# A decoder layer in one kernel: the output projection as three split passes, with its weights in the ring

## What is computed

```python
x = x + attn(layernorm(x), W_Q, b_Q, W_K, b_K, W_V, b_V, W_O, b_O)
x = x + xattn(layernorm(x), k, fside, ctx, ctx, 8)
x = x + ffn(layernorm(x), ...)

def attn(x, ...):
    Q, K, V = x @ W_Q + b_Q, x @ W_K + b_K, x @ W_V + b_V   # per head, float32
    scores = rope(Q) @ rope(K).T / sqrt(128)
    probs = softmax(where(causal, scores, -inf))
    z = probs @ V
    return einsum('bqnd,ndm->bqm', z, W_O) + b_O
```

## Time and profile before

| | us |
|---|---|
| timed runs, median of 3 | 995.27 (993.92 to 996.04) |
| the profiled execution | 985.83 |
| its span | 983.8 |
| TensorE busy in the span | 949.0 |
| VectorE, ScalarE, GpSimd busy | 723.6, 379.0, 408.5 |

### The profile page before, as it was taken

How to read it: one execution, slowest core, us unless ns; L and a number is a source line. 1 busy time by engine, 2 the same in 40 slices (tenths; PEclk the granted TensorE clock), 3 DMA queues, 4 the chain that set the end, 5 groups by cost and what they waited for, 6 DMA issues and landing times.

```text
span 983.8 us, 18292 instructions
## 1 busy us (share of the span) xinstructions
PE 949.0 (96%) x6081; PEld 836.6 (85%) x6081; DVE 723.6 (74%) x1523; ACT 379.0 (39%) x1063; POOL 408.5 (42%) x320
## 2 busy tenths in 40 slices
PE   7999999999999999999999999888999999999996
PEld 6788888988898888888898888777888799999985
DVE  6878967877877889667888777646777666666647
ACT  3546443442234643233544333431352344444420
POOL 1312313163521245563225365306706366666660
PEclk9999999999999999999999999989999999999999
DMA  7863397321079922236877501350142477777768
GB/s 268 306 238 138 118 354 288 147 87 65 1 246 368 356 87 72 80 103 219 298 261 244 198 35 45 135 233 26 67 172 78 95 121 121 119 118 120 119 113 297
DMA packets 64841, 161.17 MB, mean 164 GB/s; under 512 B 6640, under 2 KB 40304, under 8 KB 63600
## 3 DMA queue, kind: packets, MB, share of 16 engines
q1 hardware_dynamic: 50304, 140.97, 40.6%
q0 software_dynamic: 14448, 19.05, 11.9%
HBM read 84.72 MB, written 75.27 MB: 163 GB/s over the span
## 4 chain that ended last, share of the span: by engine, by line
PE 86%; issue 4%; DVE 4%; POOL 2%; ACT 2%; DMA 1%; SPq 0%; DVEq 0%; ACTq 0%
PE bank L487 12%; PE bank L489 11%; PE bank L488 11%; PE bank L717 11%; PE bank L735 6%; PE bank L567 6%; PE bank L863 4%; PE bank L865 3%; PE bank L553 3%; PE bank L590 3%; PE bank L592 3%; PE bank L591 2%; POOL xs L1208 2%; PE bank L834 2%; PE bank L824 2%
## 5 line engine op out<-in xcount | busy, mean ns | idle before, releaser
L1200 POOL TENSOR_TENSOR rot<-turn 128x512 f32<-128x512 f32 x64 | 94.2, 1472 | 283.6 <-DVE rtotal L1357 216.2
L1368 DVE SCALAR_TENSOR_TENSOR turn<-bank,bqk,trig 128x1024 f32<-128x1024 f32 x128 | 162.2, 1279 | 29.0 <-PE bank L489 26.0
L1263 POOL DMA_INDIRECT sums<-ysb,token_at x79 | 123.1, 1558 | 69.5 <-DVE ysb L1736 35.2
L1230 POOL TENSOR_TENSOR kv<-c_t,v_t 128x512 f32<-128x512 f32 x64 | 67.8, 1071 | 134.6 <-PE bank L592 69.0
L717 PE MATMUL bank<-wo,z_t 128*128 128x256 f32 x512 | 116.0, 379 | 0.8 <-ACT z_t L1066 0.8
L487 PE MATMUL bank<-xt_hi,w_hi 128*128 128x512 f32 x256 | 105.3, 411 | 1.7 <-DVE xt_lo L1332 1.7
L717 PEld LDWEIGHTS bank<-wo,z_t 128*128 128x128 f32 x512 | 94.9, 190 | 12.8 <-ACT z_t L1066 1.0
L1058 ACT COPY prob_t<-bank 128x512 f32<-128x512 f32 x64 | 37.5, 586 | 163.3 <-PE bank L553 163.3
L489 PE MATMUL bank<-xt_hi,w_lo 128*128 128x512 f32 x256 | 100.1, 391 | 0.0
L1024 ACT ACTIVATE prob<-prob,negmax 128x128 f32<-128x128 f32 x256 | 99.0, 390 | 2.5 <-DVE negmax L1353 2.4
L488 PE MATMUL bank<-xt_lo,w_hi 128*128 128x512 f32 x256 | 99.7, 390 | 0.0
(11 more groups left out here) (181 smaller groups left out, 2285.7 us busy)
## 6 DMA issues: line engine op xcount, KB each, us to landing
xs<-zeros SPq DMA_DIRECT2D x16, 2120.0 KB, 13.6
w_hi<-w_dram SPq DMA_DIRECT2D x24, 768.0 KB, 4.3
w_lo<-w_dram SPq DMA_DIRECT2D x24, 768.0 KB, 7.2
xe_all<-xs SPq DMA_DIRECT2D x79, 132.5 KB, 2.6
sums<-zeros SPq DMA_DIRECT2D x3, 2176.0 KB, 18.3
raw<-in_wqkv SPq DMA_DIRECT2D x16, 384.0 KB, 4.2
w_dram<-w_hi SPq DMA_DIRECT2D x8, 768.0 KB, 6.6
w_dram<-w_lo SPq DMA_DIRECT2D x8, 768.0 KB, 8.5
```

The source lines that it names most:

```text
L1200: nc.gpsimd.tensor_tensor(rot[m][1][:], turn[m][1], turn[m][2], ALU.add).then_inc(rot_pool, 1)
L1263: nc.gpsimd.indirect_dma_start(sums_dram[s % SUMS], bass.IndirectOffsetOnAxis(ap=token_at[:, s:s + 1], axis=0), ysb[s % YBUFS][:], None, c ...
L1368: last = nc.vector.scalar_tensor_tensor(turn_all[m][:, 2 * i:2 * i + 2, :], qk_bank[2 * m + i][:].unsqueeze(1).to_broadcast([128, 2, GT]), ...
```

## The change

- The output projection becomes three fp32r passes over z_hi, z_lo, wo_hi and wo_lo: 24 matmuls of 256 columns in a step.
- ScalarE writes the weighed values with their bias to prob_t, which it has just finished with, and casts them from there to z_hi. GpSimd subtracts to get z_lo (`z_low`), first thing in its step. ScalarE's next copy into prob_t waits for it.
- wo is no longer loaded in whole. Two heads of it (128 x 512) are a third chunk of each pair's weights, in the same raw buffers; the list CHUNKS gives the order. The chunk that comes with pair q belongs to the output projection of pair q - 2. It is stored with the pair (wo_dram) and loaded again with it, so a pair is now 2 MB where it was 1.5 MB. The reload of a place waits for the output projection too. Two more loads come in the tail.
- Of the four kv products of a step of GpSimd the last two move into the next step, behind the low parts.

```diff
+CHUNKS = [(0, 0), (0, 1), (1, 0), (1, 1), (0, CH), (1, CH)] + [(p, c) for p in range(2, PAIRS) for c in range(CH + 1)]
             for p in range(PAIRS):
-                for c in range(CH):
+                while n < len(CHUNKS) and CHUNKS[n][0] <= p and (p or CHUNKS[n] in ((0, 0), (0, 1))):
+                    q, c = CHUNKS[n]
                     if n >= 2:
                         sp.wait_ge(w_hi_done, n - 1)
                         sp.wait_ge(w_lo_done, n - 1)
-                    sp.dma_start(raw[n % 2][:], wqkv_in[p, c]).then_inc(raw_loaded[n % 2], 16)
+                    if c < CH:
+                        sp.dma_start(raw[n % 2][:], wqkv_in[q, c]).then_inc(raw_loaded[n % 2], 16)
+                    else:
+                        sp.dma_start(raw[n % 2][:, 0:2 * D], wo_in[wo_pair(q)]).then_inc(raw_loaded[n % 2], 16)
                     n += 1
...
                     sp.wait_ge(v_ready, 2 * (PAIRS * (g - 1) + W_BEFORE[p] + 1))
+                    sp.wait_ge(wo_done, PAIRS * (g - 1) + W_BEFORE[p] - 1)
...
+                    load_wo(p)
...
-                    pe.wait_ge(zt_taken, s * 2 - 4)
...
+                    at = W_AT[(p - 1) % PAIRS]
+                    pe.wait_ge(z_hi_done, s * 2 - 4)
+                    pe.wait_ge(z_lo_done, s * 2 - 4)
...
                         for h in range(2):
-                            last = nc.tensor.matmul(
-                                acc[b // 2][:, (b % 2) * D:(b % 2 + 1) * D], z_t[h][:, b, :],
-                                wo[:, 2 * r + h, :], start=(r == 0 and b % 2 == 0 and h == 0),
-                                stop=(r == PAIRS - 1 and h == 1), skip_group_check=True)
+                            nc.tensor.matmul(o, z_hi[h][:, b, :], wo_hi[:, at, h, :],
+                                             start=(r == 0 and b % 2 == 0 and h == 0), stop=False, skip_group_check=True)
+                            nc.tensor.matmul(o, z_hi[h][:, b, :], wo_lo[:, at, h, :],
+                                             start=False, stop=False, skip_group_check=True)
+                            last = nc.tensor.matmul(o, z_lo[h][:, b, :], wo_hi[:, at, h, :], start=False,
+                                                    stop=(r == PAIRS - 1 and h == 1), skip_group_check=True)
...
-                                act.wait_ge(zt_ready, s * 2 - 6 + h + 1)
+                                act.wait_ge(z_lo_done, s * 2 - 6 + h + 1)
...
-                            nc.scalar.activation(z_t[h][:], zt_bank[:].rearrange("p (b n) -> p b n", b=GB),
+                            nc.scalar.activation(prob_t[h][:], zt_bank[:].rearrange("p (b n) -> p b n", b=GB),
                                                  ACT.Identity, bias=bv[:, n:n + 1]).then_inc(zt_taken, 1)
...
+                            nc.scalar.copy(z_hi[h][:], prob_t[h][:]).then_inc(z_hi_done, 1)
...
                 if first and p < PAIRS - 1:
-                    split_hi(2 * p + 2)
-                    split_hi(2 * p + 3)
+                    for n in range(3 * p + (3 if p else 2), 3 * p + 6):
+                        split_hi(n)
...
+            def z_low(g, p, live):
+                s = g * PAIRS + p
+                for h in range(2):
+                    pool.wait_ge(z_hi_done, s * 2 - 4 + h + 1)
+                    nc.gpsimd.tensor_tensor(z_lo[h][:], prob_t[h][:], z_hi[h][:].bitcast(F32),
+                                            ALU.subtract).then_inc(z_lo_done, 1)
+
             def core_step(g, p, live, first):
                 s = g * PAIRS + p
+                if live(2):
+                    z_low(g, p, live)
+                    if g > 0 and live(0) and 3 <= p < 7:
+                        for f in range(2, 4):
+                            cross_kv(g - 1, 4 * (p - 3) + f)
...
-                    for f in range(4):
+                    for f in range(2):
                         cross_kv(g - 1, 4 * (p - 2) + f)
...
                 if first and p < PAIRS - 1:
-                    split_lo(2 * p + 2)
-                    split_lo(2 * p + 3)
+                    for n in range(3 * p + (3 if p else 2), 3 * p + 6):
+                        split_lo(n)
```

More of the change, by code:

```diff
@@ L56, with wo_pair @@
 EARLY = EXPERTS // 2
+CHUNKS = [(0, 0), (0, 1), (1, 0), (1, 1), (0, CH), (1, CH)] + [(p, c) for p in range(2, PAIRS) for c in range(CH + 1)]
+def wo_pair(q):
+    return (q - 2) % PAIRS
 def shared_bank(k, i):
@@ L150, in decoder @@
         prob_t = [sb(f"prob_t{h}", [128, GB, SEQ], c=tctx) for h in range(2)]
-        z_t = [sb(f"z_t{h}", [128, GB, SEQ], c=tctx) for h in range(2)]
-        wo = sb("wo", [128, HEADS, D], c=tctx)
+        z_hi = [sb(f"z_hi{h}", [128, GB, SEQ], F32R, tctx) for h in range(2)]
+        z_lo = [sb(f"z_lo{h}", [128, GB, SEQ], F32R, tctx) for h in range(2)]
+        wo_hi = sb("wo_hi", [128, WRING, 2, D], F32R, tctx)
+        wo_lo = sb("wo_lo", [128, WRING, 2, D], F32R, tctx)
         bqk = sb("bqk", [128, PAIRS, 4], c=tctx)
@@ L231, in decoder @@
         small_loaded = sem("small_loaded")
-        wo_loaded = sem("wo_loaded")
+        z_hi_done = sem("z_hi_done")
+        z_lo_done = sem("z_lo_done")
         raw_loaded = [sem(f"raw_loaded{i}") for i in range(2)]
@@ L426, in _ @@
                         sp.dma_start(ctxg[:], ctx_in[:, g * GB:(g + 1) * GB, :]).then_inc(ctx_loaded, 16)
+            for p in range(2):
+                sp.wait_ge(wo_done, PAIRS * (GROUPS - 1) + W_BEFORE[p] - 1)
+                load_wo(p)
             sp.wait_ge(v_ready, 2 * PAIRS * GROUPS)
@@ L969, in split_hi @@
                 act.wait_ge(raw_loaded[n % 2], 16 * (n // 2 + 1))
-                p = n // CH
-                if p >= WRING and n % CH == 0:
-                    act.wait_ge(w_stored[W_AT[p]], 32 * W_NTH[p])
+                p, c = CHUNKS[n]
+                if p >= WRING and c == 0:
+                    act.wait_ge(w_stored[W_AT[p]], 64 * W_NTH[p])
                     act.wait_ge(v_ready, 2 * (p - WRING) + 2)
-                nc.scalar.copy(w_hi[:, W_AT[p], n % CH, :], raw[n % 2][:]).then_inc(w_hi_done, 1)
+                if c < CH:
+                    nc.scalar.copy(w_hi[:, W_AT[p], c, :], raw[n % 2][:]).then_inc(w_hi_done, 1)
+                else:
+                    if p > WRING + 1:
+                        act.wait_ge(wo_done, p - WRING - 1)
+                    nc.scalar.copy(wo_hi[:, W_AT[p]], raw[n % 2][:, 0:2 * D].rearrange("p (h n) -> p h n", h=2)).then_inc(w_hi_done, 1)
             def route_exp(g):
@@ L1319, in split_lo @@
                 dve.wait_ge(w_hi_done, n + 1)
-                at = W_AT[n // CH]
-                nc.vector.tensor_tensor(w_lo[:, at, n % CH, :], raw[n % 2][:],
-                                        w_hi[:, at, n % CH, :].bitcast(F32), ALU.subtract).then_inc(w_lo_done, 1)
+                p, c = CHUNKS[n]
+                at = W_AT[p]
+                if c < CH:
+                    nc.vector.tensor_tensor(w_lo[:, at, c, :], raw[n % 2][:], w_hi[:, at, c, :].bitcast(F32),
+                                            ALU.subtract).then_inc(w_lo_done, 1)
+                else:
+                    nc.vector.tensor_tensor(wo_lo[:, at], raw[n % 2][:, 0:2 * D].rearrange("p (h n) -> p h n", h=2),
+                                            wo_hi[:, at].bitcast(F32), ALU.subtract).then_inc(w_lo_done, 1)
             def step(g, p, live, first):
```

46 lines of the change are left out of this document (28 added, 18 removed).

## The result

| | before | after |
|---|---|---|
| timed runs, median | 994.6 us | 1047.23 us (1046.52 to 1048.23) |
| ratio after to before | | 1.0533 [1.0517, 1.0549] |
| the profiled execution, its span | 985.83, 983.8 us | 1048.23, 1046.1 us |

The change costs 52.6 us. The forecast was 26.8 us, with a range that ended at 1040 us: right in sign, half the size.

The account below looks back on a forecast made before the run. TensorE, a full queue from 50 to 620 us, was taken as the bound. Group 0's stall +29.4, clock +10.5, gain -14.5 and tail +1.4 made +26.8 us on a median of 995.27: 1022.1 us, range 1003 to 1040.

Parts of the forecast that it names:

- The stall of group 0: Group 0: the third chunk's load waits for a raw buffer, holding ScalarE's copy and TensorE; +29.4 us before the clock.
- The clock: Group 0: TensorE's idle gaps lower its clock; 1.75 us for each of six waits, +10.5 us, bounds 0 and 20.
- 21.1 us: Group 0: forecast step length, from one transposition of the probabilities to the next, against 16.89 us before.
- I cost it at nothing: Group 0: raw loads A or B queued behind longer stores and loads have almost a whole step; 0 us.
- Rival 2: Group 0's wait is there, but the clock holds or the load lands at 2.4 us: 1010 us; chance 0.22.
- rivals 1 and 4: 1: wait hidden, gain comes through, 981 us, chance 0.08. 4: half the wait covered, 993 to 997 us, chance 0.03.
- GpSimd in the steps with scatters: Groups 2 and 3, steps 5 to 7: added low parts just fit before the rotation; zero, other end +1 us each.
- The gain: Output projection: 24 passes take 2.88 us instead of 3.46; 0.58 us a step, -14.5 us over 25 steps.
- I count 24 + 1 = 25: Steps credited with the shorter output projection: 24 in groups 1 to 3, one in the tail; none in group 0.
- TensorE has other waits there: Tail: the last output projections' wait for cast and subtraction doesn't decide; gus_hi on ScalarE moves back, +1.4 us.
- The forecast profile: Signs: ScalarE idle before wo_hi, TensorE idle at low clock, group 0 longer, groups 1 to 3 shorter, shorter output projection.
- Rival 3: Heavier: load lands at 4.2 us (+9.6), clock (+10) or GpSimd late (+6); two together 1038 to 1048; chance 0.17 over 1033.

Follow-up runs that it names:

- e2: The changed kernel with a third raw buffer, alive only in group 0: 999.6 us, ratio 1.0045 to the kernel before.
- e5: The changed kernel with 16 more matmuls in each of steps 2 to 7 of group 0, ahead of TensorE's wait: 1035.77 us, ratio 1.0429.
- e3: The changed kernel with GpSimd's wait for scattered rows moved behind z_lo in groups 2 and 3: 1034.77 us, ratio 1.0401.
- e4: The changed kernel with both a third raw buffer and the wait for scattered rows behind z_lo: 986.01 us, ratio 0.9912.
- e8: The changed kernel with third raw buffer and moved wait for scattered rows, run again in more rounds: 984.73 us, ratio 0.9915.
- e6: The kernel before, with the wait for scattered rows moved behind the next step's first rotation in groups 2 and 3: 990.41 us, ratio 0.9968.
- e1: The kernel before, unchanged, profiled once more: 994.84 us, ratio 0.9997.

## Why the prediction was wrong

It added up to +26.8 us, and +52.6 was measured. Three terms carry the difference.

**The stall of group 0: mechanism right, +39.9 forecast (29.4 and 10.5 for the clock), 47.6 measured at T(8).** What came true: T(2) 43.69 (forecast 44.1), the landing 2.8 us (2.6), the cast and the copy behind it, TensorE's wait of 4.6 to 6.9 us (4.8), and removal of the one cause removes all of it (e2). Size by size:
- The clock, 10.5 us forecast, about 15 measured. After each of the six waits TensorE worked its first 4.7 to 5.6 us at a granted clock of 0.50, the 1.2 GHz level; one of them, window from T(3) on:

```profile
67.01:72.32 5.31, 5.31 (x39) 4.75 (x40) 0.57 (x2) 0.59 (x1) 0.00 (x0) 0.50 0.96 382
```

  In sum that is 31.7 us, of which half, 15.8, is an upper estimate of the loss. Two steps that e5 ran at whole clock were 2.5 us shorter each, and six times that is 15. The prediction had read 3.4 us for one such stretch and took half, since "Part of a low stretch may pass while TensorE is still idle, and a shorter one would lose half of that". The stretches were no shorter (the one above is at 0.50 from 65.49 to 72.32), and only 1.3 to 2.1 us of each lay in the wait.
- Step 5 to 6, which e5 runs at whole clock in 25.21 us against a forecast of 21.1: +4.1. There VectorE computes the moments of all later tokens. In the kernel before most of this work stood in time that VectorE had free (18.09 against 16.89). After, VectorE comes to it only behind wo_lo, when everybody already waits. Timeline of VectorE after:

```profile
113.96 0.69 DVE L1378 TENSOR_TENSOR wo_lo<-raw,wo_hi 128x512 fp32r<-128x512 f32 x1 [2.80 <-ACT wo_hi L1012]
114.57 4.01 DVE L1337 BATCH_NORM_STATS2 stats<-x 128x6 f32<-128x256 f32 x12
118.48 0.90 DVE L1340 BATCH_NORM_AGGREGATE mv<-stats 128x2 f32<-128x6 f32 x12
```

  The prediction made 21.1 us from one step and multiplied it. The old T in the earlier trace rows already had an odd one, 85.26 to 103.35, and that was the place to ask what lies behind the new wait.
- The 21.1 us themselves hold. e5 has 22.0 from T(3) to T(4), and there ScalarE had waited 5.13 us for the raw load of the first chunk, so that VectorE stood idle for 0.70 us ahead of its low parts. In the changed kernel, with its slower TensorE, ScalarE waited 2.91 us for that load and VectorE not at all, so "I cost it at nothing" was right there.

With T(2) 0.4 us earlier than forecast, and a last step to T(8) that is 0.5 us shorter at whole clock than in the kernel before, the four make 4.5 + 4.1 - 0.4 - 0.5 = 7.7 us. Rival 2, that the clock holds, falls, and so do rivals 1 and 4.

**GpSimd in the steps with scatters: 0 forecast, +6 as the other end, 12.5 measured (e3).** This is the step that failed most. "It just fits" fails in two ways.
- The sum was too short even for a step with prompt rows. The kernel after has one from 444.89 on, ahead of T(22). From the kv that TensorE releases to the first rotation it takes 13.3 us, and the forecast (401.55 to 413.7) had 12.15: the low parts took 2.5 us for 2.2 and the two kv behind them 3.0 for 2.2. TensorE waits 0.27 us for the product and 0.74 for the rotation.
- It took one scatter's duration with its wait from the earlier trace rows, a step in group 2, as a constant, and stated in one clause that z_lo is ready ahead of the output projection. It is in that step. It isn't in group 3, where zeros and reloads run beside the scatter (2.66 us of idle TensorE ahead of T(30)), nor behind the scatter of step 7 (5.56 us ahead of T(33)), where the old kernel had 6.46 us of idle time in front of GpSimd's next work and the new one has z_lo.

The new dependence of TensorE on GpSimd's program order was seen as work to be fitted in, and not as a wait that anything ahead of it may lengthen.

**The gain: -14.5 us and +1.4 in the tail forecast, about -9 measured (e4, e8), -6 beside e6.** The size of one was right: 24 passes in 2.88 us, steps of 16.31 for 16.89 and 21.21 for 21.81 us. By the rule of a quarter (the Trainium skill, FP8 and Floating Point Precision, section TensorE Precision Notes, as the prediction cites it) they would have fallen by 0.86 us; the measurement decides for 0.58: an fp32r pass takes 0.12 us, and a quarter of the float32 product 0.108 (3.46 / 32). What failed is "I count 24 + 1 = 25". In e8 the first step with convolutions in a group (T(11) to T(12) 20.83 for 20.74, T(19) to T(20) 20.98 for 20.88) and the steps T(23) to T(24), T(30) to T(31) and T(31) to T(32) are no shorter, since TensorE isn't what is late in them: it waits 0.45 us in the step from T(19), 0.79 and 0.80 us for ScalarE's prob_t in those from T(23) and T(31), 0.74 us for the rotation in the one from T(30). The tail had another wait than the forecast one, which was gus_hi with +1.4 us. From T(32) to T(33) e8 takes 13.20 us for 10.40, +2.8, because the output projection waits for the cast and the subtraction; "TensorE has other waits there" is what failed. TensorE in e8:

```profile
623.25 0.55 PE L751 MATMUL bank<-wo_hi,z_hi 128*128 128x256 f32 x1 [2.82 <-issue]
```

And the front costs: T(2) is 1.6 to 3.3 us later in e2, e4 and e8 than before, for the two chunks of wo that are cast there.

Together: 26.8 + 7.7 + 12.5 + 4 = 51 us. The missing 1.6 us are within what single executions differ by (e1). The last two terms depend on what they are compared with: if the 3 us that the move gives the kernel before (e6) are taken out of both, GpSimd's order cost 9 us and the gain fell short by 7.

The forecast profile was mostly there: ScalarE idle ahead of wo_hi (4.2 to 8.7 us, forecast 3 to 5), TensorE idle 5 us with a clock under 1, group 0 longer (47.6 us, forecast 25 to 40), an output projection of 2.9 us. Missed: groups 1 to 3 gave 13 to 15 us in the forecast, and took 4 (T(8) to T(32)). Rival 3 came nearest, with 1038 to 1048 us for two of its causes. Its GpSimd was there at twice its size and its clock at half the surplus it named; its load that lands at 4.2 us was not.

## What to carry to other kernels

When an engine's work becomes an operand of the bottleneck engine, everything ahead of it in that engine's program becomes a wait of the bottleneck: a wait for one's own DMA that did little harm there must move behind the new work. Adding one more item per step to a ring that held exactly the items of a step turns a prefetch into a round trip; count the buffers against the items before the passes. And a stall is never only its own length: it drags the clock down and bares work that stood in its neighbours' free time, so price each step of the pipeline, not one and a multiple.
